# One-core encoder block: the first sequence's U copies on ScalarE, another load order, G and U in other places

## The reference

```python
# 1: conditioned bottleneck; its weights depend on the sequence
h = x + relu(x @ (down_project * (c @ down_gamma) + c @ down_beta)) @ (up_project * (c @ up_gamma) + c @ up_beta)
# 2: attention on binary paths; 8 heads, depth 5, causal
paths = sigmoid(h @ Wp + bp)
agree = pq * pk + (1 - pq) * (1 - pk)
sim = cumprod(agree, -1).sum(-1) / 5
x = x + (softmax(where(mask, -inf, sim)) @ (h @ Wv)) @ Wo
# 3: low-rank conditioned map, and an expert choice on top
U = (c @ W_dec + b_dec).reshape(B, 257, 30)
y = x @ (U[:, :-1] @ V) + U[:, -1:] @ V
x = x + y + expert_w[argmax(y @ gate_w.T)] @ y
```

## Time and profile before

| | us |
|---|---|
| median of 3 runs | 150.49 |
| lowest and highest | 150.21, 151.03 |
| the profiled execution | 150.6 |
| its span in the trace | 148.9 |
| TensorE busy | 138.3 |
| VectorE busy | 99.5 |
| ScalarE busy | 56.3 |
| GpSimd busy | 49.0 |

### The profile page before, as it was taken

The page is one execution under the profiler, slowest core; times in us unless marked ns, Lnnn a source line. Parts: engine busy times, 40 slices in busy tenths (PEclk is TensorE's granted clock), DMA queues, the critical chain, the costliest instruction groups (busy, mean ns, idle before and its releaser), DMA issues.

```text
span 148.9 us, 4940 instructions
## 1 busy us (share of the span) xinstructions
PE 138.3 (93%) x2190; PEld 87.3 (59%) x2190; DVE 99.5 (67%) x186; ACT 56.3 (38%) x67; POOL 49.0 (33%) x71
## 2 busy tenths in 40 slices
PE   5999679999988999999899999999999998999992
PEld 5646346655535577665565766556557674667651
DVE  0473737883998746689957567699376967984431
ACT  3013370544543132558414344473235466310010
POOL 7200056006062632453075336600665651200000
PEclk9999999999998699999999999999999999999999
DMA  4999999910022000000011100011011010111212
GB/s 108 324 362 424 409 358 350 317 39 0 2 33 31 6 4 4 0 4 0 0 40 42 35 2 4 4 35 40 0 35 40 4 35 7 35 38 37 70 39 72
DMA packets 7381, 12.62 MB, mean 85 GB/s; under 512 B 1552, under 2 KB 5808, under 8 KB 7232
## 3 DMA queue, kind: packets, MB, share of 16 engines
q1 hardware_dynamic: 7120, 11.86, 22.8%
q0 software_dynamic: 96, 0.05, 0.8%
q10 hardware_dynamic: 144, 0.39, 0.7%
HBM read 10.09 MB, written 2.22 MB: 83 GB/s over the span
## 4 chain that ended last, share of the span: by engine, by line
PE 69%; DVE 19%; issue 5%; POOL 3%; ACT 3%; DVEq 0%; POOLq 0%; ACTq 0%
PE work L656 37%; PE c_ps L656 16%; PE s_ps L656 12%; DVE tiles L596 3%; DVE rden L481 2%; DVE feat L646 2%; DVE tiles L599 2%; ACT prob L428 2%; PE work L787 2%; POOL zo L411 2%; PE work L847 2%; DVE phi_t L546 1%; DVE h_t L529 1%; PE work L839 1%; DVE tiles L592 1%
## 5 line engine op out<-in xcount | busy, mean ns | idle before, releaser
L428 ACT ACTIVATE prob<-s_ps 128x1536 f32<-128x1536 f32 (+1 forms) x24 | 38.3, 1594 | 41.5 <-PE s_ps L656 41.5
L392 POOL TENSOR_SCALAR_AFFINE_SELECT prob<-prob 128x1024 f32<-128x1024 f32 x16 | 18.0, 1127 | 70.1 <-ACT prob L428 70.1
L481 DVE RECIPROCAL rden<-c_ps 128x256 f32<-128x256 f32 x16 | 28.1, 1754 | 6.7 <-PE c_ps L656 6.7
L656 PE MATMUL s_ps<-phi_t 32*128 32x256 f32 (+1 forms) x384 | 24.1, 365 | 1.1 <-DVE phi_t L546 0.6
L656 PEld LDWEIGHTS s_ps<-phi_t 32*128 32x128 f32 x384 | 17.4, 184 | 11.7 <-issue 8.5
L656 PE MATMUL c_ps<-prob,v_sb 128*32 128x256 f32 (+1 forms) x384 | 22.8, 356 | 0.0
L404 POOL TENSOR_TENSOR short<-prob 128x512 f32<-128x512 f32 x15 | 20.2, 1346 | 1.3
L656 PE MATMUL work<-ctx_t,mix_sb 128*32 128x256 f32 x256 | 17.0, 381 | 0.5 <-ACT zo_t L463 0.2
L656 PE MATMUL work<-zo_t,gexp 128*32 128x256 f32 x256 | 16.9, 379 | 0.0
L656 PEld LDWEIGHTS c_ps<-prob,v_sb 128*32 128x32 f32 x384 | 11.0, 111 | 9.0 <-issue 3.2
L656 PE MATMUL work<-w_vl,h_t 128*32 128x296 f32 x208 | 15.1, 415 | 0.4 <-DVE h_t L529 0.4
(11 more groups left out here) (109 smaller groups left out, 154.2 us busy)
## 6 DMA issues: line engine op xcount, KB each, us to landing
wdec<-in_W_dec SPq DMA_DIRECT2D x1, 3855.0 KB, 18.3
x_t<-in_x_tr SPq DMA_DIRECT2D x4, 512.0 KB, 9.0
ex_t<-in_expert_tr SPq DMA_DIRECT2D x1, 2048.0 KB, 25.3
out_x<-x_t SPq DMA_DIRECT2D x16, 128.0 KB, 1.7
mix_sb<-in_mix SPq DMA_DIRECT2D x1, 904.0 KB, 19.9
lift_sb<-in_lift ACTq DMA_DIRECT2D x1, 384.0 KB, 4.0
w_vl<-in_vl SPq DMA_DIRECT2D x1, 296.0 KB, 5.2
first_sb<-in_first SPq DMA_DIRECT2D x1, 144.0 KB, 3.6
```

Of the source, the lines that this page charges most:

```text
L392: nc.gpsimd.affine_select(out=tri, in_=tri, compare_op=ALU.is_ge, fill=0.0, base=0, pattern=[[0, HG], [0, 2], [1, P]], channel_multiplier= ...
L428: nc.scalar.activation(prob[:, p % 2, :, 0:width(p)], s_ps[:, :, 0:width(p)], ACT.Exp).then_inc(exped, 1)
L481: link(nc.vector.reciprocal(rden[:], c_ps[m % 2][:, CW:2 * CW]))
L656: return nc.tensor.matmul(o, w, r, start=start, stop=stop, skip_group_check=True)
```

## The change

It moves steps in the list, changes the engine of some copies and the order of the loads; what is computed stays the same.

- ScalarE copies ("U", 0), ("U", 1), ("U", 2) and both "lift" steps out of PSUM, which VectorE did.
- Of the phi copies of whole sequences, ScalarE does both for sequence 1, and the second (g = 1) rather than the first for sequences 2 and 3.
- `lift_sb` is loaded on SP's queue, second in order. `mix_sb` and `ex_t` come ahead of `wdec`.
- ("G", 0) goes into the head, before the first phi; ("G", 1) follows context 0. Q stands with ugT in the gap after scores 2.
- U starts later: ("U", 0) after context 2, ("U", 1) before and ("U", 2) after context 3, ("U", 3) after context 4. SP waits for each piece that another engine copied.
- phi of the second half of sequence 0 and its feat go into the head. "ubT" follows context 5.
- The first addition of a chunk's denominators stands just before its context, behind the gap's steps, and no longer before its scores.

```diff
--- before.py
+++ after.py
@@ -99,7 +99,9 @@
 
 def scaler(s):
 
-    return "scalar" if s[2] == 0 and s[3] != SECOND else "vector"
+    if s[3] == ALL_T:
+        return "scalar" if s[2] == 1 or s[1] == 1 else "vector"
+    return "scalar" if s[2] == 0 and s[3] == FIRST else "vector"
 
 
 def features(b, ts):
@@ -109,10 +111,10 @@
 
 PROLOGUE = [("gdn", (0,)), ("gup", 0), ("down", 0), ("gdn", (1, 2, 3)), ("up", 0, 0), ("up", 0, 1), ("gup", 1),
             ("VL", 0, 0), ("VL", 0, 1), *features(0, FIRST), ("feat", 0, FIRST), ("VL", 0, 2), ("VL", 0, 3), ("bias", 0, SECOND),
-            ("phi", 0, 0, FIRST), ("phi", 0, 1, FIRST), ("tanh", 0, SECOND), ("scores", 0), ("feat", 0, SECOND),
-            ("down", 1)]
+            ("G", 0), ("phi", 0, 0, FIRST), ("phi", 0, 1, FIRST), ("tanh", 0, SECOND), ("scores", 0),
+            ("down", 1), ("feat", 0, SECOND), ("phi", 0, 0, SECOND), ("phi", 0, 1, SECOND)]
 EARLY_BANK = {("gdn", (0,)): 0, ("gup", 0): 1, ("down", 0): 2, ("gdn", (1, 2, 3)): 3, ("up", 0, 0): 4, ("up", 0, 1): 5,
-              ("gup", 1): 0, ("VL", 0, 0): 1, ("VL", 0, 1): 2, ("VL", 0, 2): 4, ("VL", 0, 3): 5,
+              ("gup", 1): 0, ("VL", 0, 0): 1, ("VL", 0, 1): 2, ("VL", 0, 2): 4, ("VL", 0, 3): 5, ("G", 0): 0,
               ("phi", 0, 0, FIRST): 1, ("phi", 0, 1, FIRST): 2}
 
 
@@ -126,10 +128,9 @@
         gaps[3] += [("feat", n1, ALL_T)]
         gaps[4] += [("phi", n1, 0, ALL_T), ("phi", n1, 1, ALL_T)]
     if b == 0:
-        gaps[0] = [("phi", b, 0, SECOND), ("phi", b, 1, SECOND)] + gaps[0]
-        gaps[1] += [("ugT",), ("U", 1)]
+        gaps[1] += [("ugT",), ("Q",)]
         gaps[2] += [("VL", n1, 2), ("VL", n1, 3)]
-        gaps[3] += [("lift", 2), ("U", 3)]
+        gaps[3] += [("lift", 2), ("U", 1)]
         gaps[5] += [("lift", 3), ("Uadd",)]
     elif n1 < B:
         gaps[1] += [("zs", prv, ALL_T), ("zo", prv, 0), ("zo", prv, 1), ("VL", n1, 1)]
@@ -147,11 +148,13 @@
     n1, n2, prv = b + 1, b + 2, b - 1
     gaps = [[] for _ in range(BP)]
     if b == 0:
-        gaps[0] += [("U", 0)]
+        gaps[0] += [("G", 1)]
         gaps[1] += [("VL", n1, 0), ("VL", n1, 1)]
-        gaps[2] += features(n1, ALL_T) + [("U", 2)]
-        gaps[4] += [("G", 0), ("ubT",), ("Q",)]
-        gaps[5] += [("down", n2), ("G", 1)]
+        gaps[2] += features(n1, ALL_T) + [("U", 0)]
+        gaps[3] += [("U", 2)]
+        gaps[4] += [("U", 3)]
+        gaps[5] += [("ubT",)]
+        gaps[5] += [("down", n2)]
     else:
         gaps[0] += [("zT", prv, ALL_T)]
         gaps[3] += [("out", prv, 0)]
@@ -177,9 +180,12 @@
         _p = _b * BP + _i
         if _p + 1 < ALL:
             ORDER += [("scores", _p + 1)]
-        ORDER += _a + [("context", _p)]
+        ORDER += _a
+        if opening(_p):
+            ORDER += [("add", _p)]
+        ORDER += [("context", _p)]
         ORDER += _c
-        if _p + 1 < ALL and long(_p + 1):
+        if _p + 1 < ALL and long(_p + 1) and not opening(_p + 1):
             ORDER += [("add", _p + 1)]
 ORDER += [("zT", B - 1, SECOND), ("out", B - 1, 0), ("zs", B - 1, SECOND), ("zo", B - 1, 1),
           ("out", B - 1, 1), ("zoT", B - 1, 1), ("out", B - 1, 2), ("out", B - 1, 3)]
@@ -333,17 +339,20 @@
         def _(sp):
 
             sp.dma_start(first_sb[:], first).then_inc(ld_first, 16)
+            sp.dma_start(lift_sb[:], lift).then_inc(ld_lift, 16)
             sp.dma_start(x_t[:, 0], x_tr[0].rearrange("(c p) t -> p c t", p=P)).then_inc(ld_x[0], 16)
             sp.dma_start(w_vl[:], vl.rearrange("p (c n) -> p c n", c=DC)).then_inc(ld_vl, 16)
             sp.dma_start(x_t[:, 1], x_tr[1].rearrange("(c p) t -> p c t", p=P)).then_inc(ld_x[1], 16)
-            sp.dma_start(wdec[:], W_dec).then_inc(ld_wdec, 16)
             sp.dma_start(mix_sb[:], mix).then_inc(ld_mix, 16)
             sp.dma_start(ex_t[:], expert_tr.rearrange("e (c p) f -> p e c f", p=P)).then_inc(ld_ex, 16)
+            sp.dma_start(wdec[:], W_dec).then_inc(ld_wdec, 16)
             for b in range(2, B):
                 sp.dma_start(x_t[:, b], x_tr[b].rearrange("(c p) t -> p c t", p=P)).then_inc(ld_x[b], 16)
             for s in ORDER:
                 if s == ("U", 3):
 
+                    done(sp, ("U", 2))
+                    done(sp, ("U", 1))
                     done(sp, s)
                     for j in range(4):
                         sp.dma_start(u_dram[:, U_COLS * j:U_COLS * (j + 1)], u_row[KP * j:KP * j + B, 0:U_COLS]
@@ -414,7 +423,6 @@
 
         @block.scalar
         def _(act):
-            act.dma_start(lift_sb[:], lift).then_inc(ld_lift, 16)
             for s in ORDER:
                 if s[0] == "scores":
                     p = s[1]
@@ -450,6 +458,14 @@
                     full(act, s)
                     nc.scalar.activation(phi_t[:, b % 2, g, tok], bank(s)[:, tok], ACT.Copy, scale=rootc[:]
                                          ).then_inc(empty(s), 1)
+                elif s[0] == "U" and s[1] < 3:
+                    m = s[1]
+                    full(act, s)
+                    nc.scalar.copy(u_row[:, U_PIECE * m:U_PIECE * (m + 1)], bank(s)[:, 0:U_PIECE]
+                                   ).then_inc(empty(s), 1)
+                elif s[0] == "lift":
+                    full(act, s)
+                    nc.scalar.copy(w_up[:, s[1], :], bank(s)[:, 0:D]).then_inc(empty(s), 1)
                 elif s[0] == "zT":
                     _, b, ts = s
                     rows = slice(KP * ts[0], KP * (ts[-1] + 1))
@@ -512,9 +528,6 @@
                                                           ug_col[:, c, b:b + 1], ug_col[:, DC + c, b:b + 1],
                                                           op0=ALU.mult, op1=ALU.add)
                         ins.then_inc(lift_ready, 1)
-                elif kind == "lift":
-                    full(dve, s)
-                    nc.vector.tensor_copy(w_up[:, s[1], :], bank(s)[:, 0:D]).then_inc(empty(s), 1)
                 elif kind == "gup":
                     b = s[1]
                     dve.wait_ge(ld_lift, 16)
@@ -558,9 +571,8 @@
                         nc.vector.tensor_tensor(ub_row[:, :, 0:K],
                                                 bank(s)[0:B, U_PIECE:U_PIECE + K].unsqueeze(1).broadcast_to([B, TT, K]),
                                                 bdec_row[:].unsqueeze(1).broadcast_to([B, TT, K]), ALU.add)
-                    full(dve, s)
-                    nc.vector.tensor_copy(u_row[:, U_PIECE * m:U_PIECE * (m + 1)], bank(s)[:, 0:U_PIECE]
-                                          ).then_inc(empty(s), 1)
+                        nc.vector.tensor_copy(u_row[:, U_PIECE * m:U_PIECE * (m + 1)], bank(s)[:, 0:U_PIECE]
+                                              ).then_inc(empty(s), 1)
                 elif kind == "ubT":
                     full(dve, s)
                     nc.vector.tensor_copy(ub_col[:], bank(s)[:, 0:B]).then_inc(empty(s), 1)
```

## The result

The changed kernel takes 160.8 us (median of 4, 159.2 to 164.0) against 150.41 us: 1.065 times as long, with a 95% interval of 1.056 to 1.074. The prediction was 160.8, with a range of 155.0 to 164.0. The ratios leave out runs that took over 1.5% longer than the fastest of their kernel, here the one of 164.04 us. Measured again later, the same kernel took 161.91 us, 1.074 (1.069 to 1.079). The profiled execution took 160.96 us, its span 159.2.

A forecast was written before the change was run, and what follows sets the result against it. TensorE, busy 138.3 of 148.9 us, was taken as the bound, so its added waits and low-clock stretches add up: 150.6 + 3.9 + 1.2 + 0 + 3.5 + 1.6 + 0 = 160.8 us, range 155.0 to 164.0.

The forecast's parts named there:

- The two waits: TensorE waits for the experts' load ahead of the first G (+3.9 us) and for U's return ahead of WoU (+3.5).
- the two low stretches: Low clock after each TensorE wait: over the head's transposes and scores (+1.2 us), and from WoU on (+1.6).
- part 1: Head: the first half of G waits for the experts' weights until 19.2, so the transposes begin 3.9 us later.
- part 2: Head: TensorE's idle time ahead of G lowers the clock over transposes, scores of pair 0 and down: +1.2 us (0 to 1.7).
- part 3: From the head to U's last piece: moved work and shorter waits balance, +0.1 us counted as nothing (-1 to +1).
- part 4: Ahead of WoU: U starts later, its 8.2 us trip through DRAM returns too late, WoU starts 3.5 us later (2.5 to 4.5).
- part 5: From WoU on: after 7 us idle the clock is low, costing 1.6 us (1.0 to 2.7).
- part 6: Later sequences: a phi copy changes engine in three of them and precedes the first denominator addition; 0 +- 0.5 us.
- Rival (b): Head: experts' weights land sooner, at 17 us or before, so the wait shrinks; 157.5 or 156.0 us in all; chance 0.22.
- the bank's part: At WoU: its bank is shared with ubT, so it waits for reciprocal, ctx_t and ub_col after Uadd, 2.4 us.
- (d): At 44 to 46: relieved VectorE keeps up, TensorE never waits, clock stays up; 147.4 us; chance 0.03.
- the lateness of the first x behind lift: Start of the head: lift's load on SP's queue delays x by about one issue, 0.43 us, covered by the experts' wait.

The follow-up runs named there:

- the filler matmuls: Changed kernel plus identity matmuls nobody reads: eight ahead of the first G, 161.33 us; in another run 24 behind the scores of pair 7, 159.42 us.
- the version without both holes: Kernel before with only the engine changes, early phi and later first addition; G, U, Q, ubT and loads unmoved: 147.97 us (147.5 to 148.9).
- run 24: This name is not in the text given; the only run with a 24 put 24 identity matmuls ahead of WoU in the changed kernel: 159.42 us.

## Why the prediction was right, step by step

The two waits and the two low stretches that the prediction names are all there, and taking them out one by one shows them to be the loss. That the sum met the median of 160.8 to the last digit is luck: the sizes of the clock's terms were off in opposite directions, and they differ from one execution to the next. The terms, on the clock of the first trace:

| step | predicted | measured |
|---|---|---|
| experts' load lands | 19.2 (18.7 to 19.6) | 18.9 (18.6 to 19.9 in eight profiles of this load order) |
| part 1: transposes begin | +3.9 | +3.6 |
| parts 2 and 3: to the last piece of U | +1.2 and 0: 48.1 | 48.37 |
| part 4: U's way through DRAM | 8.2 | 8.07 |
| WoU begins | 52.75 + 8.6 = 61.35 | 61.28 |
| part 5: clock behind WoU | +1.6 (1.0 to 2.7) | +1.2 to +1.3 (+2.6 to +3.6 in four other profiles) |
| part 6: later sequences | 0 +- 0.5 | +0.5 |

**Part 1** was right in mechanism and size. The landing, put at 19.2, came 0.3 us sooner in this trace; but in three of the eight profiles it came at 19.8 to 19.9, above the upper end of 19.6. Rival (b), in which they land by 17, was seen in no profile.

**Part 2** was mis-sized where it happened: the low clock in the head costs 2.2 us (9.63 against 7.43), not 1.2. I had taken one stretch as in the earlier trace rows, but it lasted twice as long. I had also lowered it for the cover that exp gives; that no run separates. **Part 3** made up for a part of it: I had counted the earlier phi as nothing, and it gave 0.7 us. The same distance, from the transposes to the step behind context 0, is 24.48 - 16.32 = 8.2 us in the kernel before and 7.4 in every profile of the new order without low clock. The line of the kernel before's timeline for that step (its first piece of U):

```profile
24.48 0.99 PE L656 MATMUL work<-wdec,first_sb 128*32 128x480 f32 x8
```
At U's last piece 0.3 us of that are left: without low clock it runs 26.2 us behind the transposes (46.65 - 20.42 in the second profile of the changed kernel), where the first half of G had run 26.5 us behind them (42.85 - 16.32). So part 2 was 1.0 too small and part 3 some 0.4 too large; together they were 0.5 too small (28.4 us from the transposes to U's last piece in the first trace, 27.9 by the prediction), and part 1, 0.3 too large, brings U's last piece to within 0.3 us of the predicted place.

**Part 4** was right to 0.1 us, with the bank's part of it shown by ubT ahead of Uadd (1.9 of the predicted 2.4 us), and the whole of it by putting U back: WoU without a wait.

**Part 5** was right in kind, as the filler matmuls show, but its size is no constant. From WoU's start to the end of the span it takes 96.7 us at full clock. In the first trace it took 97.9, and in the four other profiles with this wait 99.3, 99.6, 100.2 and 100.3: the low clock costs 1.2 us in one and 2.6 to 3.6 in the others, three of these above my end of 2.7. The second profile of the changed kernel lost nothing in the head and 2.9 us here, the first 2.2 and 1.2: 2.9 and 3.4 us in all, where parts 2 and 5 together had 2.8. So the sum held because the stretches traded places.

**Part 6**: from context 6 (+9.8) to the end of the span (+10.3) another 0.5 us came in, at the end of my range. It has nothing to do with the waits. The kernel with only the changes of engine has it too: 96.7 us from WoU's start to the end, against 96.2 in the kernel before (148.9 - 52.75), both at full clock. Which of the moved copies or the later addition it is, no run separates.

The rival on the other side, (d), describes what half of the change does: with its moves of G, U and the loads undone it gave 148.0 us, where (d) had 147.4; the 0.5 us of part 6 are most of the difference. It needed both waits gone, as said, and neither was.

**One step was wrong without harm**: the lateness of the first x behind lift. I had about 0.43 us for it; the first trace had 1.3. The wait for the experts covered it. Alone, it cost 0.4 to 0.5. It also made the idle time ahead of the first G shorter than predicted, 2.06 us and not 3.6.

## What to carry to other kernels

Before a step moves up to fill a small hole, add up when its operands land behind everything issued ahead of them: here a hole of 0.76 us was filled with a step whose data came 3 us later, and the wait stood in the order of all that followed. Before the producer of a long round trip moves down, count the trip (8 us) from its new place to its reader, and look at what shares the reader's bank and stands behind the wait on the evicting engine. Of a change with several parts, run the parts alone: one half of this one was worth -1.6%, the other cost over 8%. And before a small gain is booked, such as the 1.07 us of G that left the later place, look at whether another path, here U's round trip, ends at the same point.

## What the runs showed of the hardware

The length of TensorE's idle time does not say by itself whether the clock falls, nor for how long. After 2.06 us idle in the head it was low for 6.8 us; after 2.91 us in the same place of the same program, in another execution, it did not fall. At WoU's start, after 4.5 to 7.3 us idle, it was low in all five profiles that have this wait without fillers; the work behind it lost 1.2 us in one and 2.6 to 3.6 in the four others. In the kernel before it had fallen around a gap of 1.26 us. By the Trainium skill, TensorE: Matmul & The Clock Gate (HAM oscillation), it is idle gaps past a certain length that bring the clock down; these runs show shorter gaps than the page's, of 1.26 and 2.06 us, with a fall and one of 2.91 us without, so here the measurement decides, and length alone does not tell.

In the head the low clock cost less than half of the time for which it was low: 2.2 us of 6.8. In the kernel before, the prediction read a loss of 1.7 us from 3.4 us at the lower level. Of 32 more executions of it, 29 have a mean granted clock of 0.987 to 0.989 and took 149.8 to 151.2 us, with a median of 150.7; three have 0.998 or 1.000 and took 149.8 to 149.9 us. An estimate from these: the fall there costs some 0.8 us. A gap of 1 to 3 us should be priced with a chance, and the program's times scatter with it: 159 to 165 us for the changed kernel, against 149.8 to 151.2 before and 147.5 to 148.9 for the version without both holes, whose profile has a granted clock of 1.00 throughout.

The landing of one and the same load moved by 1.3 us between the eight profiles of the new load order (18.6 to 19.9), and that of the first x by 1.8 us between those with lift ahead of it (6.3 to 8.1 us). The profiles come from several chips; on one of them, two kernels with the same head, profiled side by side, had the experts' load land at 18.6 and 19.3. A program that waits for a load inherits this; before, no wait of TensorE ended with a load.
